# Layer 1 of a two-layer relational graph attention kernel: eleven Strassen pairs and three plain tiles instead of ten and five, with q's edge work moved among the products

## The chip, the cores and the metric

One core of one Trainium2 chip. The time is the device time of one execution in microseconds (us); where several runs are told of, their median. TensorE (PE) does matrix products and transposes, VectorE (DVE), ScalarE (ACT) and GpSimd (POOL) work element by element, SyncE (SP) issues transfers. Each engine works its own list of instructions in order and waits for others by semaphores.

## The reference, cut to what matters

N = 3125 nodes of 768 numbers, E = 53125 edges (src, dst, one of R = 3 relations), float32 throughout. Two attention layers, a residual and a layer norm. Layer 1 has H = 4 heads of 192 columns, layer 2 one head of 768:

```python
xr = einsum('nd,rdf->rnf', x, W)              # every node by each relation's 768x768 matrix
qi, kj = xr[etype, dst] @ q, xr[etype, src] @ k
alpha = leaky_relu(qi + kj, 0.2)
e = exp(alpha - segment_max(alpha, dst)[dst])
out = segment_sum(e / z[dst] * xr[etype, src], dst) + b      # z: sum of e over a node's edges
h = elu(layer1(x)); out = layernorm(x + layer2(h))
```

## The kernel before, in words

**Tiles.** Nodes stand in NT = 25 tiles of 125. Edges, sorted by dst, are padded into 440 steps of 128, and for the softmax they lie as 110 rows of 512 (`ROWS`, `RL`), each row on a partition.

**The tables.** Before xr is known, each node's q and k scores for the three relations come from x times (W q) and (W k), into `qk_node`. POOL scatters the q part, one indirect transfer for each of the 25 tiles (`q_scattered`), into a table in DRAM of zeros, one line of 12 numbers (3 relations x 4 heads) an edge. SP then loads that table whole (`big<-q_fill`, 110 rows of 512 x 12 numbers), and DVE spreads it over the edges: `q_ends` runs one scan over each of the 12 columns, PE turns the rows' last values (`turn_q_ends`), DVE carries them from row to row (`q_carries`), PE turns them back (`turn_q_carry`), and `q_of_edges` adds them in by 12 instructions of 512 columns, masks each relation's four columns by the edge's relation (3 of 2048) and sums the relations into `alpha` (2 of 2048).

**The product phase of layer 1** makes xr. `PLAINS` tiles are done plainly by `dense`: six units (3 relations x 2 halves of 384 columns), each of 6 products over chunks of 128 rows. The other tiles go in `PAIRS`, two at a time, by Strassen's scheme: for each relation 7 products of 3 chunks (`product`), written as A11, S2, S1, A12, S3, S4, A22 in the order list `ORDER`, interleaved so that two relations overlap; a pair is a turn of 21 products (j = 0 to 20 in the first). The scheme needs sums of the pair's four quarters (`sum_x`, four DVE instructions of 375 columns) and of each relation's weight quarters (`sum_w`, three of 1152 columns, and `sum_w_in_place`, one). After each product ACT copies it out (A11, A12) or DVE adds it to what is there (`add_product`, all others); PE's next product into the same bank waits for that: S3 for the add of S2, S4 for that of S1, A22 for that of S3, S2 of the relation after next for that of A22.

In layer 1 the five plain tiles come first. PE runs `turn_rows` in tile 0 and, in tile 3, `turn_q_ends` behind unit 0 and `turn_q_carry` behind unit 2. After tile 4 it waits for `qcarry_taken` and enters the pairs. DVE does in this order: `q_ends`, `sum_w(0)`, `q_carries`, `q_of_edges`, `found_tiles` (14 small instructions), `sum_w` of relations 1 and 2, one `place_hot`, `sum_x(0)`, the sums in place, and then goes along `ORDER`. Between products PE also looks up k values by one-hot products (`look_up`, 24 groups of three, one group in seven products), and DVE picks from them (`select`). POOL meanwhile gathers the other k values from the k table, paced by the count of units and products done (`units_before`).

**The row phase of layer 1**: for 440 steps POOL gathers rows of xr, ACT makes weighted one-hots, PE multiplies, DVE adds into `big`.

**Between the layers**: DVE divides tile t by its softmax sum and adds b + 1 (`divide`), ACT takes exp (`exp_hidden`), DVE forms the ELU (min, max), PE turns the tile (`x_turn`), ACT copies it (`take`), PE makes its q and k (`flat_products`, `flat_turn`), ACT copies those (`take_flat`, `take_nodes`). This is a loop over five turns of U = 5 tiles. ACT stores the k table of five tiles at a time (`store_k`), SP stores the turned tiles (`store_xT`). Layer 2 then goes as layer 1 with 1 plain tile, 12 pairs and one head.

## Time and profile before

| what | us |
|---|---|
| three runs | 2480.73, 2479.11, 2479.05; median 2479.11 |
| the profiled execution: time, span | 2475.89, 2474.2 |
| TensorE busy | 2410.9 (97%) |
| VectorE busy | 1366.4 (55%) |
| ScalarE busy | 1042.4 (42%) |
| GpSimd busy | 1611.6 (65%) |
| mean granted TensorE clock | 0.992 of full speed |

The span runs from the first instruction to the last. Line numbers are those of the kernel before.

### The profile page before, as it was taken

How to read it: one execution, taken by the hardware profiler on the slowest of the kernel's cores; microseconds unless marked ns; L12 is line 12 of the kernel's file. 1: busy time of each engine (PE TensorE's matmuls, PEld its weight loads, DVE VectorE, ACT ScalarE, POOL GpSimd, SP SyncE). 2: the span in 40 equal slices, each digit the busy share in tenths (PEclk: the TensorE clock that was granted, in tenths of full speed). 3: DMA queues.
4: the chain of work that ended last, by engine and by line, in shares of the span. 5: the costliest groups of instructions: out<-in, count | busy, mean ns of one | idle time of the engine just before them, and what ended most of it. 6: DMA issues, size and time to landing. Idle time of an engine off the chain costs nothing.

```text
span 2474.2 us, 42371 instructions
## 1 busy us (share of the span) xinstructions
PE 2410.9 (97%) x10155; PEld 1664.5 (67%) x10155; DVE 1366.4 (55%) x2669; ACT 1042.4 (42%) x2950; POOL 1611.6 (65%) x1672
## 2 busy tenths in 40 slices
PE   8999999999999999999989999999997999999998
PEld 4555666665599999999976566665554555555554
DVE  7537665655588888888897543332331332233232
ACT  0111000000099999999974000000002566666664
POOL 1377777777377777777736766667714777777774
PEclk9999999999999999999999999999999999999999
DMA  7652334332299999999843233322226999999996
GB/s 280 213 141 55 98 103 113 99 83 66 63 315 331 314 312 321 316 312 323 296 146 100 67 87 90 89 73 79 72 68 190 342 337 345 341 337 343 340 332 235
DMA packets 163568, 505.15 MB, mean 204 GB/s; under 512 B 54505, under 2 KB 60178, under 8 KB 163349
## 3 DMA queue, kind: packets, MB, share of 16 engines
q0 software_dynamic: 96048, 354.41, 42.7%
q1 hardware_dynamic: 54449, 143.18, 17.7%
q10 hardware_dynamic: 12962, 6.14, 1.1%
q8 instruction: 63, 1.03, 0.2%
q14 instruction: 46, 0.38, 0.0%
HBM read 424.00 MB, written 79.54 MB: 204 GB/s over the span
## 4 chain that ended last, share of the span: by engine, by line
PE 89%; DVE 4%; DMA 2%; POOL 2%; issue 2%; ACT 0%; ACTq 0%; DVEq 0%; SPq 0%; POOLq 0%
PE banks L1022 36%; PE banks L1064 23%; PE banks L1088 11%; PE banks L1084 11%; PE banks L930 2%; PE banks L732 1%; PE banks L907 1%; POOL q_fill L1472 1%; PE banks L925 1%; PE banks L767 1%; DMA big<-q_fill 1%; PE banks L725 1%; POOL ring L1510 1%; PE banks L743 1%; DVE ring L1552 1%
## 5 line engine op out<-in xcount | busy, mean ns | idle before, releaser
L1510 POOL DMA_INDIRECT ring<-xr_table,row_idx x704 | 667.4, 948 | 303.0 <-PE banks L1064 96.4
L1485 POOL DMA_INDIRECT big<-k_table,row_idx x700 | 687.9, 983 | 259.8 <-issue 208.0
L1286 ACT ACTIVATE work<-work,wE 128x125 f32<-128x125 f32 x1760 | 552.0, 388 | 35.2 <-DVE work L1987 19.5
L1022 PE MATMUL banks<-work 128*125 128x384 f32 x1548 | 534.1, 488 | 1.4 <-DVE work L1840 1.4
L1064 PE MATMUL banks<-ring,work 128*125 128x193 f32 x2816 | 471.4, 327 | 7.5 <-ACT work L1286 7.5
L1064 PEld LDWEIGHTS banks<-ring,work 128*125 128x125 f32 x2816 | 465.0, 188 | 7.7 <-issue 7.7
L2004 DVE TENSOR_TENSOR big<-big,banks 125x772 f32 x440 | 421.7, 958 | 64.9 <-PE banks L1064 55.9
L1862 DVE TENSOR_TENSOR ring<-ring,banks 125x384 f32<-125x384 f32 x330 | 182.2, 553 | 488.5 <-PE banks L1022 487.2
L1022 PEld LDWEIGHTS banks<-work 128*125 128x125 f32 x1548 | 283.5, 188 | 183.8 <-DVE work L1840 2.1
L1022 PE MATMUL banks<-big,work 128*125 128x384 f32 x1152 | 397.8, 487 | 0.0
L1308 ACT ACTIVATE work<-rel,wE 128x125 f32<-128x125 f32 x440 | 216.1, 491 | 234.7 <-PE banks L1088 225.1
L1022 PEld LDWEIGHTS banks<-big,work 128*125 128x125 f32 x1152 | 211.5, 188 | 136.4 <-issue 0.2
L1084 PE MATMUL banks<-ring,work 128*125 128x384 f32 x704 | 286.8, 489 | 13.0 <-DMA ring<-xr_table,row_idx 13.0
L1269 ACT COPY ring<-banks 125x384 f32<-125x384 f32 x66 | 31.6, 479 | 633.5 <-PE banks L1022 633.5
L1088 PE MATMUL banks<-ring,work 128*125 128x386 f32 x704 | 287.2, 490 | 0.0
L2064 DVE TENSOR_SCALAR small<-banks 125x1 f32<-125x1 f32 x25 | 3.9, 158 | 399.8 <-PE banks L1088 399.8
L1084 PEld LDWEIGHTS banks<-ring,work 128*125 128x125 f32 x704 | 131.9, 188 | 112.5 <-issue 18.7
L1510 POOL DMA_INDIRECT work<-xr_table,row_idx x176 | 167.0, 949 | 60.8 <-PE banks L1088 23.7
L1088 PEld LDWEIGHTS banks<-ring,work 128*125 128x125 f32 x704 | 132.2, 188 | 97.0 <-issue 4.5
L1296 ACT ACTIVATE rel<-iota_n,dloc 128x125 f32<-128x125 f32 x440 | 169.1, 384 | 9.2 <-DVEq L1978 7.4
L907 PE MATMUL banks<-work 128*125 128x384 f32 x432 | 140.5, 487 | 0.0
L1265 ACT COPY ring<-banks 125x384 f32<-125x384 f32 x66 | 31.6, 479 | 245.3 <-PE banks L1022 245.3
(282 smaller groups left out, 2005.4 us busy)
## 6 DMA issues: line engine op xcount, KB each, us to landing
xr_table<-ring SPq DMA_DIRECT2D x75, 337.8 KB
xr_table<-ring SPq DMA_DIRECT2D x75, 336.9 KB
work<-in_L_gnn_W SPq DMA_DIRECT2D x36, 384.0 KB, 7.1
ring<-xr_table,row_idx POOLq DMA_INDIRECT x704, 5.0
big<-k_table,row_idx POOLq DMA_INDIRECT x700, 2.4
work<-in_x_turned SPq DMA_DIRECT2D x25, 375.0 KB, 5.6
out<-work SPq DMA_DIRECT2D x25, 336.0 KB
work<-in_x SPq DMA_DIRECT2D x23, 336.0 KB
```

The source lines that it names most:

```text
L907: last = pe.matmul(bank[b][0:TN, 0:n_cols], xT_slot(n if l == 0 else PLAIN_TILE, TN)[:, c, :], w_cols(r, first, n_cols)[:, c, :], start=(c ...
L1022: last = pe.matmul(bank[b][0:TN, 0:HALF], left_side(l, left, pair)[:, c, :], right_side(l, left, r)[:, c, :], start=(left in ("A11", "S1", ...
L1064: last = pe.matmul(bank[2 * slot + half][0:TN, m * HW:(m + 1) * HW], one_hots[l][:, slot, h, :], row[:, half * HB2 + m * HW:half * HB2 + ( ...
L1084: pe.matmul(sums[0:TN, bass.ds(at, HALF)], one_hots[l][:, st % AHEAD, 0, :], row[:, 0:HALF], start=False, stop=False, skip_group_check=True)
L1088: pe.matmul(sums[0:TN, bass.ds(at + 512, ROWW[l] - HALF)], one_hots[l][:, st % AHEAD, 0, :], row[:, HALF:ROWW[l]], start=False, stop=False ...
L1286: last = nc.scalar.activation(one_hots[l][:, slot, h, :], hot[:, slot, :], ACT.Copy, scale=wE[:, bass.ds(st, 1), h:h + 1].rearrange("p a b ...
L1296: nc.scalar.activation(gaps[:, slot, :], iota_n[:, :], ACT.Abs, scale=-1.0, bias=dloc[:, bass.ds(st, 1)]).then_inc(s["gap_set"], 1)
L1308: nc.scalar.activation(one_hots[l][:, j % AHEAD, 0, :], gaps[:, j % AHEAD, :], ACT.Relu, scale=wE[:, bass.ds(st, 1), 1:2].rearrange("p a b ...
L1485: nc.gpsimd.indirect_dma_start(k_at(l, st), None, ktab[l], bass.IndirectOffsetOnAxis(ap=row_idx[:, st:st + 1], axis=0)).then_inc(s["k_gath ...
L1510: nc.gpsimd.indirect_dma_start(row_slot(l, st % GS), None, xrtab[l], bass.IndirectOffsetOnAxis(ap=row_idx[:, st:st + 1], axis=0)).then_inc ...
L1862: nc.vector.tensor_tensor(out_, in_, acc, ALU.add).then_inc(s["halves_out"], 1)
L2004: nc.vector.tensor_tensor(tile, tile, banks[0:TN, 2 * (j % AHEAD):2 * (j % AHEAD) + 2, 0:RWL // 2], ALU.add).then_inc(s["sum_added"], 1)
```

## The change

Layer 1 has three plain tiles and eleven pairs; the last pair is tiles 23 and 24, and pair 0 is loaded into the other slot, before the q table. All spots that are counted in products from the end move on by 21. k lookups and the loads of W2 begin one turn later. The q table is loaded in two halves (256 of each row's 512 edges), and `q_ends` scans half after half. The twelve columns are no longer written apart (`qf`): every later instruction of q works in the loaded table itself, whose neighbours of one column lie 12 numbers (48 bytes) apart. PE's turns of q's ends stand in plain tile 2, behind units 3 and 4. DVE does `sum_w(0)`, two thirds of `sum_w(1)` and `sum_x(0)` ahead of `q_ends`; `q_of_edges` stays ahead of the products, the masks and the sums of q go among the first turn's products, behind j = 2 and j = 7, the rest of the weight sums behind j = 9 to 15, `found_tiles` behind 16, and `sum_x(1)` behind 18. The wait for `qcarry_taken` ahead of the products is gone. Between the layers, b + 1 is formed before the row phase, the softmax sums of the first five tiles are inverted first, tile 0's ELU comes ahead of tile 2's division, ACT looks two tiles ahead instead of three in the first turn, and SP stores layer 2's k table. The last product is followed by one POOL memset of 1152 columns instead of one of 3456.

```diff
-    PLAINS = [U, 1]
+    PLAINS = [3, 1]
-    LOOK_FROM = [0, R]
+    LOOK_FROM = [R, R]
-    Q_ENDS_AT, Q_CARRY_AT, PLACES_FROM = 5, 9, 14
+    Q_ENDS_AT, Q_CARRY_AT, PLACES_FROM = 5, 9, [16, 14]
+    EDGES_AT, ALPHA_SPOT = 2, 7
+    W_SPOTS = [9, 11, 14, 15]
+    X_SPOTS = [18, TURN // 2 + 2]
+    W2_FROM = R
+    SUMMED = [{"S": [1, 2, 5], "S3": [3, 4, 7], "A22": [1, 6, 8]}, {"S": [9, 10, 11], "S3": [12, 13, 14], "A22": [9, 10, 11]}]
...
+                        sp.wait_ge(s["qk_copied"], 2 + U * i + U)
+                        for a, b in PARTS:
+                            sp.dma_start(ktab[l].rearrange("(t p r) h -> p t (r h)", p=TN, r=R)[a:b, bass.ds(U * i, U), :],
+                                         qk_node[a:b, bass.ds(U * i, U), R * H:2 * R * H]).then_inc(s["k_stored"], 16)
...
+                if l == 0:
+                    sp.wait_ge(s["qk_done"], 2 + WT + FLATS)
+                    load_pair(0)
                 sp.wait_ge(s["q_scattered"], 16 * NT * (l + 1))
...
+                    half = RL // 2 * R * H
+                    sp.dma_start(q_filled(l)[:, 0:half], q_rows[:, 0:half]).then_inc(s["q_loaded"], 16)
+                    sp.dma_start(q_filled(l)[:, half:], q_rows[:, half:]).then_inc(half_loaded, 16)
...
                     if k == 1:
+                        sp.wait_ge(s["dense_done"], 2 * UNITS + 2 * UNITS)
                         load_pair(1)
-                        sp.wait_ge(s["dense_done"], 2 * UNITS + 2 * UNITS)
-                        load_pair(0)
+                        for row, arr in ((q2_row, q2), (k2_row, k2)):
+                            sp.dma_start(row, arr.rearrange("f h -> (f h)").partition_broadcast(P)).then_inc(qk_loaded, 16)
...
-                    meets = {0: {2: turn_rows}, 3: {0: turn_q_ends, 2: turn_q_carry}} if l == 0 else {}
+                    meets = {0: {2: turn_rows}, 2: {3: turn_q_ends, 4: turn_q_carry}} if l == 0 else {}
                     dense(k, meets.get(k, ()))
-                if l == 0:
-                    pe.wait_ge(s["qcarry_taken"], l + 1)
...
-                        if k == 0 and not first:
-                            store_k(i - 1)
...
-                qs = qf if l == 0 else raw
+                qs = raw
...
+                    mid = RL // 2 if l == 0 else RL
                     for q in range(R * H):
-                        link(nc.vector.tensor_tensor_scan(qs[:, q, :], same[0:ROWS, :], raw[:, q, :], 0.0, ALU.mult, ALU.add))
+                        link(nc.vector.tensor_tensor_scan(qs[:, q, 0:mid], same[0:ROWS, 0:mid], raw[:, q, 0:mid], 0.0, ALU.mult, ALU.add))
+                    if l == 0:
+                        dve.wait_ge(half_loaded, 16)
+                        for q in range(R * H):
+                            link(nc.vector.tensor_tensor_scan(qs[:, q, mid:], same[0:ROWS, mid:], raw[:, q, mid:],
+                                                              qs[:, q, mid - 1:mid], ALU.mult, ALU.add))
...
                 if l == 0:
-                    place_hot(0)
-                    dve.wait_ge(s["dense_done"], 2 * UNITS + UNITS * 3)
-                sum_x(0)
-                if l == 1:
+                    sum_w(0)
+                    sum_w_firsts(1).then_inc(s["w_summed"], 1)
+                    dve.wait_ge(s["w_summed"], 2)
+                    sum_x(0)
+                    q_firsts()
+                    q_ends()
+                    sum_w_in_place(0)
+                    q_carries()
+                    sum_w_in_place(1)
+                    q_of_edges()
+                else:
...
                 for j, (left, u) in enumerate(ORDER[l]):
                     if left not in BY_ACT:
                         add_product(left, u)
-                    if j % TURN == TURN // 2 + 2 and l < j // TURN + 1 < PAIRS[l]:
+                    if j % TURN == X_SPOTS[0 if l == 0 and j < TURN else 1] and l < j // TURN + 1 < PAIRS[l]:
                         sum_x(j // TURN + 1)
+                    if l == 0 and j == EDGES_AT:
+                        q_of_relations()
+                    if l == 0 and j == ALPHA_SPOT:
+                        q_sums()
+                        dve.sem_inc(s["k_taken"], 2)
+                    if l == 0 and j == W_SPOTS[0]:
+                        sum_w_firsts(2).then_inc(s["w_summed"], 1)
+                    if l == 0 and j == W_SPOTS[1]:
+                        sum_w_last(1)
+                    if l == 0 and j == W_SPOTS[2]:
+                        sum_w_in_place(2)
+                    if l == 0 and j == W_SPOTS[3]:
+                        dve.wait_ge(s["w_summed"], SUMMED[0]["S"][2])
+                        sum_w_last(2)
...
+                    take_weights(0, U)
+                    for t in range(2):
+                        divide(t, brow[0:TN, :]).then_inc(s["u_ready"], 1)
+                    for t in range(U):
+                        activate(t, t)
+                        if t == U - 2:
+                            take_weights(U, NT)
+                        divide(t + 2, brow[0:TN, :]).then_inc(s["u_ready"], 1)
```

`sum_w_firsts` is the first two instructions of `sum_w`, `sum_w_last` the third, `q_of_relations` the three masks, `q_sums` the two sums. `take_weights(a, b)` adds a small number to the softmax sums of tiles a to b and inverts them, `activate` is the ELU's min and max.

## Rows read from the trace of the kernel before

**Rows 1.** The trace in stretches: length, busy time of each engine, clock, DMA.
```profile
core 0: us, PE busy (x) PEld busy (x) DVE busy (x) ACT busy (x) POOL busy (x), PEclk, DMA share, GB/s
210.80:214.52 3.72, 3.72 (x13) 2.22 (x12) 3.22 (x14) 1.34 (x3) 2.81 (x4) 1.00 0.44 136
...
1362.50:1877.00 514.50, 513.59 (x1743) 308.62 (x1741) 190.82 (x352) 35.54 (x74) 307.01 (x320) 1.00 0.27 78
```
**Rows 2.** Timeline of TensorE in layer 1's plain tiles: start, length, instructions, idle before.
```profile
181.01 0.25 PE L938 MATMUL banks<-ident,small 110*12 110x110 f32 x1 [2.18 <-DVE small L1687]
...
189.10 35.10 PE L907 MATMUL banks<-work 128*125 128x384 f32 x108
225.64 2.20 PE L1022 MATMUL banks<-work 128*125 128x384 f32 x6 [1.45 <-DVE work L1840]
```
**Rows 3.** The chain that ended last: start, length, what.
```profile
146.38 19.18 DMA big<-q_fill
...
1671.46 89.04 PE banks L1022 x276
```
**Rows 4.** Timeline of VectorE on q in layer 1.
```profile
165.59 15.07 DVE L1686 TENSOR_TENSOR_SCAN big<-same,big 110x512 f32<-110x512 f32 x12 [38.23 <-DMA big<-q_fill]
...
189.55 9.42 DVE L1706 SCALAR_TENSOR_TENSOR big<-big,small 110x512 f32<-110x512 f32 x12 [0.17 <-DVE small L1703]
199.00 6.95 DVE L1710 SCALAR_TENSOR_TENSOR big<-rel,big 110x2048 f32<-110x2048 f32 x3
```
**Rows 5.** VectorE by line and shape, layer 1: count, busy us, mean ns.
```profile
L1862 DVE TENSOR_TENSOR ring<-ring,banks 125x384 f32<-125x384 f32 x150 | 82.8, 553 | 174.2 <-PE banks L1022 173.3
...
L1686 DVE TENSOR_TENSOR_SCAN big<-same,big 110x512 f32<-110x512 f32 x12 | 14.7, 1224 | 38.6 <-DMA big<-q_fill 38.2
...
L1706 DVE SCALAR_TENSOR_TENSOR big<-big,small 110x512 f32<-110x512 f32 x12 | 9.0, 752 | 0.6 <-DVE small L1703 0.2
...
L1837 DVE TENSOR_TENSOR work<-work 128x375 f32<-128x375 f32 x10 | 5.5, 548 | 0.3
...
L1725 DVE TENSOR_TENSOR big<-work 128x1152 f32<-128x1152 f32 x3 | 4.1, 1355 | 0.4 <-DVE big L1746 0.3
...
L1970 DVE COPY wE<-banks 128x440 f32<-128x440 f32 x4 | 3.6, 897 | 0.4 <-DVE wE L1970 0.2
...
L1688 DVE TENSOR_TENSOR_SCAN big<-same 110x512 f32<-110x512 f32 x1 | 1.2, 1217 | 0.0
```
**Rows 6.** The same view of layer 2, 1382 to 1400 us.
```profile
L1706 DVE SCALAR_TENSOR_TENSOR big<-big,small 110x512 f32<-110x512 f32 x3 | 2.8, 929 | 0.2 <-DVE small L1703 0.2
```
**Rows 7.** Timeline of VectorE: scans of 128 columns.
```profile
593.28 1.80 DVE L1881 TENSOR_TENSOR_SCAN big<-pen,big 110x128 f32<-110x128 f32 x4
...
599.52 2.04 DVE L1881 TENSOR_TENSOR_SCAN big<-pen,big 110x128 f32<-110x128 f32 x4
```
**Rows 8.** Stretches behind layer 1's last product, columns as in rows 1.
```profile
675.70:678.00 2.30, 0.43 (x5) 0.22 (x3) 2.01 (x4) 0.00 (x0) 2.30 (x1) 1.00 0.58 181
...
680.00:683.00 3.00, 0.00 (x0) 0.00 (x0) 2.21 (x6) 1.93 (x7) 2.39 (x3) 0.73 0.51 138
683.00:684.00 1.00, 0.38 (x1) 0.39 (x2) 0.62 (x2) 1.00 (x5) 0.70 (x2) 0.50 0.71 142
...
688.00:690.00 2.00, 2.00 (x13) 2.00 (x12) 1.46 (x3) 1.10 (x5) 1.39 (x3) 0.95 0.99 326
```
**Rows 9.** Timeline between the layers.
```profile
1264.95 0.78 DVE L2013 RECIPROCAL small<-small 125x100 f32<-125x100 f32 x1
...
1266.48 4.04 DVE L2022 SCALAR_TENSOR_TENSOR big<-big,small,brow 125x192 f32<-125x192 f32 x12 [0.15 <-DVE brow L2016]
...
1271.44 1.51 PE L725 MATMUL banks<-ident,work 125*128 125x125 f32 x6 [7.90 <-DVE work L2038]
...
1294.20 1.45 PE L732 MATMUL banks<-work 128*6 128x125 f32 x12 [0.86 <-ACT qk_node L1147]
...
1332.07 1.45 PE L732 MATMUL banks<-work 128*6 128x125 f32 x12 [0.40 <-ACT qk_node L1147]
```

More of the change, by code:

```diff
@@ L1175, in x_turns @@
                             take(t + 1, (k + 1) % U)
+                        if first and k == U - 1:
+                            exp_hidden(t + 3, (k + 3) % U)
                         take_flat(t, k)
@@ L1716, in q_of_edges, with w_sums, sum_w_firsts @@
                     dve.sem_inc(s["q_used"], 1)
-                def sum_w(r):
+                def w_sums(r):
+                    return [w_sum(l, r, i) for i in range(3)]
+                def sum_w_firsts(r):
                     if l == 0:
```

175 lines of the change are left out of this document (92 added, 83 removed).

## The prediction, made before the changed kernel was run

> **What bounds the kernel now.** I read first the engines' shares, then the chain that ended last, then the timelines where the chain leaves TensorE. PE is busy for 97% of the span, and the chain runs over its products. In the product phase a product of three chunks takes 89.04 / 46 = 1.936 us [rows 3]. In the plain tiles 108 recorded products take 35.10 us, so a tile (72 of them) takes 23.4 us and one of its six units 3.90 us [rows 2]. So time is to be won only by taking work from PE or by filling its gaps. Around the change there are three gaps: 2.18 us at the turn of q's ends and 1.45 us ahead of the pairs [rows 2], and, between the layers, a late start and four short stalls [rows 9]. The reader should also see how near q's work stands to the path: the table's load takes 19.18 us from 146.38 [rows 3], DVE waits for it and then scans for 15.07 us [rows 4]. Until now plain tiles of PE covered nearly all of that.
>
> **Part 1, PE's own work.** Two plain tiles go, 46.8 us; one pair comes, 21 products, 40.7 us: -6.1 us. The two old gaps go with the place they stood in: -3.6 us. Together -9.8 us (rounded terms). The 24 groups of lookups only move.
>
> **Part 2, the wait in plain tile 2.** Counting units back from 178.83 (where PE fell idle, 2.18 us before 181.01 [rows 2]), unit 3 of tile 2, three units earlier, ends at 178.83 - 3 x 3.90 = 167.1. PE then waits for `qend_ready`. The load begins when the scatters are through, as before. If its halves land evenly, the first is there at about 156.0 and the second at 165.6 [rows 3]. A scan of 128 columns takes 0.45 us with a constant and 0.51 us with a tensor as its first value [rows 7], one of 512 takes 1.256 with its gap [rows 4]; between them, 256 columns take 0.72 and 0.78. The first half is scanned by 164.6, the second from 165.6 to 174.9, and with the copy 174.7 to 175.1 is the time of the ends. PE waits 7.5 us (7.6 to 8.0 by this sum, less if the second half lands sooner). Lower bound: the table wholly there by 152, then DVE alone needs 18 us, 170.2, a wait of 3.1; upper bound 8.3. Behind PE's wait stand units 4 and 5 and the whole product phase; DVE's `q_of_edges` waits behind unit 4 as well.
>
> **Part 3, the clock.** Behind layer 1's last product PE falls idle at about 676.1. From 680 to 683 its mean clock is 0.73, so it went from 2.4 to 1.2 GHz at about 681.4, after 5 us; PE resumes at 683.62, and is at 2.4 GHz again at about 688.2 [rows 8]. Those 4.6 us at half speed cost 2.3 us. A wait of 7.5 us is longer than those 5 us: +2.3 us. With a wait under 5 us it is nothing.
>
> **Part 4, the first turn of pairs.** Here DVE gets new work at a new price: q's instructions read and write numbers 48 bytes apart. A plain instruction of 1152 columns takes 1.355 us and one of 375 takes 0.548, so 1.04 ns a column and 0.16 fixed [rows 5]. A step of 12 bytes (layer 2) takes 0.929 instead of 0.752 for 512 columns [rows 5, 6], 0.35 ns a column more. A copy that writes 440 numbers 16 bytes apart takes 0.897 us, 1.68 ns a column, 0.64 more [rows 5]. No row shows such an instruction at 48 bytes except the scan, which reads at that step for 1.224 against 1.217 [rows 5]; but it needs 2.1 ns a column anyway and can hide the step. I take the price of 16 bytes, the nearest row. Then, with old prices in brackets [rows 4]: twelve of `q_of_edges` 13.2 to 13.4 us (9.42), three masks 10.9 (6.95), two sums 7.3 (4.6 at the masks' rate).
>
> The Trainium skill bears on this (Advanced Engine Details and Errata, Memory Cachelines): SBUF has lines of 16 bytes, and an access pattern that goes to another line with each access pays. By it 48 bytes should cost what 16 bytes cost; by the scan's row the step would be free. The first gives the sum below, the second the 3.8 us named beside it.
>
> Now the walk, in us from the first product's start; a product 1.94, an add 0.55, `sum_x` 2.3, two thirds of a weight sum 2.7, one third 1.4 [rows 3, 5]. The carries are turned one unit earlier, -3.9; DVE ends `q_of_edges` at 9.7. S3 (j = 4, due at 7.7) needs the add of S2: 10.3, a stall of 2.5. The masks run from 10.8 to 21.8, then the add of S3; A22 (j = 9, due at 20.0) starts at 22.4: 2.4. Two adds, the sums of q to 30.8, two adds, two thirds of `sum_w(2)` to 34.6; S2 of the third relation (j = 13, due at 30.1): 4.5. The last product of the turn ends at 46.2; DVE has just finished `found_tiles` (3.7 us [rows 1]) and one-hots, adds that product (that alone must follow it) and does `sum_x(1)`: A11 of pair 1 starts at 49.8: 3.6. Sum +13.0 us. At 12 bytes' price the same walk gives 8.4, at the contiguous one 3.8, nearly all `sum_x(1)` behind j = 18. None of these stalls reaches 5 us, so no clock is lost. Layer 1's front: -9.8 + 7.5 + 2.3 + 13.0 = +13.0 us.
>
> **Part 5, between the layers.** DVE does three tiles' divisions (12 in 4.04 us) before the first ELU; now two, -1.35. Inverting 20 numbers instead of 100 saves 0.6 of 0.78 us and its gap, and b + 1 leaves the 0.75 us between that and the first division: PE's first turn comes 2.5 us sooner, the second tile's 2.3, and from there PE runs on [rows 9]. Given back: ACT makes up its extra exp at the first turn's end, and DVE inverts the other 80 numbers there: +0.6, an estimate between nothing and 1.3. The four stalls of PE behind ACT's k stores (0.86 to 0.40, first and last in rows 9, four in all, 3.0 us) go, with 0.2 us of refilling. Sum -5.0 us (-3 to -6.5). b + 1 now stands between the last product and the first one-hots; ACT has its first set ready 1.2 us before PE starts at 683.62 on the first gathered rows, which covers it; without that cover it is +0.6. SP's k stores make the next turned tile wait a tile or so, but its slot is wanted five tiles later: nothing. The shorter memset: POOL then waits for the last stores anyway: nothing. The last sixteen k gathers are let go 14 products (27 us) before PE turns them instead of 17, and keep POOL busy for 16 us by the page (983 ns each): nothing, but with less to spare. The later q2 and k2 rows are read three groups later than before: nothing.
>
> **Sum.** +13.0 - 5.0 = +8.0 us on the profiled execution (2475.89, span 2474.2), 2483.9. The three runs shown have a median of 2479.11, 3.2 above that one; the change is set against the median: **2487.1 us**.
>
> **The rivals.** (a) The step costs only what 12 bytes cost: front -9.8 + 7.5 + 2.3 + 8.4 = +8.4, total +3.4, 2482.5. For it: no row shows more at a small step. Against it: the 16-byte copy. Chance 0.2. (b) The step is free, as for the scans: +3.8 in the turn, total -1.2, 2477.9. Chance 0.12. (c) The other side: the products have room for all of q's work, so that turn 1 costs nothing, total 8.0 - 13.0 = -5.0, or somewhat below, since a late DVE would then also be no reason for `sum_x(1)` to hold PE: 2474 and less, faster. For it: layer 2 does the same edge work among its products, and PE is busy there for 513.59 of 514.50 us [rows 1]. Against it: that is one head's work, 3 columns and not 12. It decides from where the turn's stalls stay under 0.5 us in all; at the walk's contiguous price they are already 3.8. Chance 0.13. (d) The step of 48 bytes is dearer than one of 16, 2 ns a column: some 2 us more on `q_of_edges`, 2 on the masks and 1.3 on the sums, of which the walk passes on nearly all, total about +13, 2492. Chance 0.1. The forecast itself keeps 0.45.
>
> **Numbers.** A change under 0.2% (5 us) can't be told from none by this kernel's measurement. Faster: (c) and a little of (b), 0.15. Same: (a), most of (b), the lower end of the forecast, 0.35. Slower: 0.5. Range 2474 to 2492: from (c)'s edge to (d). The likeliest case's own range, from the bounds of the wait, the clock and part 5, is 2481 to 2491.
>
> **What would show it.** In the profile after: PE idle behind a plain unit at about 167 until about 175, released by DVE's copy of the ends, and half clock behind it; `q_of_edges` near 1.1 us each and the masks near 3.6; stalls of PE in the first turn at its fifth, tenth, fourteenth and twenty-second product; the row phase starting 13 us later; then the first turned tile 2.5 us nearer to the row phase's end, no stall at each fifth tile. Wrong if the masks take 2.3 us, if the table lands well before 160, or if the first turn shows no stall.

## The result and the profile after

The changed kernel takes 2494.96 us (median of six runs, 2492.03 to 2498.96) against 2479.72 for the kernel before in the same job: ratio 1.0066, 95% interval 1.0056 to 1.0076, so +16.4 us, slower. The profiled execution took 2498.96 us, its span is 2497.2, its mean clock 0.984. It is the slowest of the six, and the profile of before is one of the faster ones.

First the timeline of PE behind plain tile 2 and in the first turn of pairs (start, length, what, and in brackets the idle time before it and who ended it); it answers to [rows 2]. L956 turns q's ends, L925 are the plain tiles, L1038 the products, L948 the lookups.

```profile
181.42 0.34 PE L956 MATMUL banks<-ident,small 110*12 110x110 f32 x1 [8.14 <-DVE small L1709]
181.55 6.06 PE L925 MATMUL banks<-work 128*125 128x384 f32 x12
...
203.09 5.59 PE L1038 MATMUL banks<-work 128*125 128x384 f32 x12 [3.52 <-DVE ring L1895]
...
215.60 2.17 PE L1038 MATMUL banks<-big,work 128*125 128x384 f32 x6 [1.11 <-DVE ring L1895]
...
228.03 6.78 PE L1038 MATMUL banks<-big,work 128*125 128x384 f32 x12 [4.45 <-DVE big L1759]
...
246.27 3.48 PE L1038 MATMUL banks<-work 128*125 128x384 f32 x6 [3.73 <-DVE work L1873]
249.54 4.49 PE L1038 MATMUL banks<-big,work 128*125 128x384 f32 x12
...
255.81 0.67 PE L948 MATMUL banks<-qk_node,big 125*128 125x300 f32 x2
```

PE waits 8.14 us for the ends, and in the turn 3.52, 1.11, 4.45 and 3.73 us ahead of its fifth, tenth, fourteenth and twentieth product, 12.8 us in all. The second thing to see is what stands behind the waits: twelve recorded products take 4.03 us at full clock (4.14 in the plain tiles), but 6.06 behind the wait for the ends and 5.59 and 6.78 behind two of the waits in the turn, and six take 3.48 instead of 2.10. The stretches of the same timeline show the clock (length, busy time by engine, then PE's granted clock, 1.00 being 2.4 GHz and 0.50 being 1.2):

```profile
181.40:187.60 6.20, 6.18 (x14) 3.27 (x14) 3.00 (x5) 0.00 (x0) 4.98 (x5) 0.66 0.05 1
203.09:208.60 5.51, 5.51 (x13) 3.20 (x14) 5.47 (x3) 0.00 (x0) 4.90 (x3) 0.73 0.02 0
228.03:234.70 6.67, 6.67 (x13) 3.65 (x14) 2.23 (x3) 0.00 (x0) 5.15 (x6) 0.60 0.16 33
246.27:249.60 3.33, 3.33 (x7) 1.84 (x8) 0.00 (x0) 0.00 (x0) 2.72 (x3) 0.62 0.06 2
```

DVE's groups by shape from 150 to 262 us (busy time, mean ns of one, idle before) answer to [rows 4] and [rows 5]:

```profile
L1731 DVE SCALAR_TENSOR_TENSOR big<-big,small 110x512 f32<-110x512 f32 x12 | 13.8, 1152 | 0.6 <-DVE small L1728 0.2
L1737 DVE SCALAR_TENSOR_TENSOR big<-rel,big 110x2048 f32<-110x2048 f32 x3 | 11.5, 3822 | 0.1
...
L1742 DVE TENSOR_TENSOR big<-big 110x2048 f32<-110x2048 f32 x1 | 3.8, 3823 | 0.0
L1744 DVE TENSOR_TENSOR big<-big 110x2048 f32<-110x2048 f32 x1 | 3.8, 3817 | 0.0
```

At the 48-byte step `q_of_edges` takes 1.15 us an instruction (0.75 before), a mask 3.82 (2.3), a sum 3.82 (2.29): 0.75 to 0.78 ns a column more than contiguous, so about 1.8 ns instead of 1.04.

A place that I had not looked at is POOL's scatters of q, while DVE does the sums that were moved ahead of `q_ends`. Timeline of both engines:

```profile
132.56 1.36 DVE L1758 TENSOR_TENSOR big<-work 128x1152 f32<-128x1152 f32 x1
132.82 2.16 POOL L1487 DMA_INDIRECT q_fill<-qk_node,start_at  x1 [0.30 <-issue]
...
135.28 1.18 POOL L1487 DMA_INDIRECT q_fill<-qk_node,start_at  x1 [0.30 <-issue]
135.35 1.36 DVE L1764 TENSOR_TENSOR big<-work,big 128x1152 f32<-128x1152 f32 x1
...
136.62 1.35 DVE L1758 TENSOR_TENSOR big<-work 128x1152 f32<-128x1152 f32 x1
136.77 2.26 POOL L1487 DMA_INDIRECT q_fill<-qk_node,start_at  x1 [0.30 <-issue]
```

The two scatters that began 0.26 and 0.15 us behind the start of one of DVE's sums of 1152 columns took 2.2 us instead of 1.19; the one at 135.28, which began 0.07 us ahead of a sum, took 1.18, and that sum its usual 1.36. From the first product of the plain tiles to the issue of q's load there are 46.7 us (106.00 to 152.69); before there were 43.8 (102.61 to 146.38).

Between the layers, the chain that ended last (start, length, what) has the row phase and layer 2's plain tile here, and PE's timeline its first turned tile:

```profile
710.01 579.96 PE banks L1080 x3520
...
1361.49 23.42 PE banks L925 x72
```

```profile
1295.42 1.51 PE L743 MATMUL banks<-ident,work 125*128 125x125 f32 x6 [5.46 <-DVE work L2092]
...
1307.41 0.86 PE L743 MATMUL banks<-ident,ring 125*128 125x125 f32 x6 [0.71 <-DVE ring L2092]
...
1310.92 0.86 PE L743 MATMUL banks<-ident,work 125*128 125x125 f32 x6 [1.06 <-DVE work L2092]
```

From the row phase's start to layer 2's first plain unit: 651.5 us, before 655.5 (683.62 to 1339.15): -4.05. PE's wait ahead of the first turned tile is 5.46 us instead of 7.90 [rows 9].

So the two traces, whose spans differ by 23.0 us, part like this: 3.4 us up to the first plain product, 22.8 from there to the first lookup behind the first turn (149.8 us against 127.0), nothing from there to the end of PE's last instruction of layer 1's product phase (446.5 in both), -3.9 from there to layer 2's first plain product, +0.7 behind it.

### The profile page after: what moved, and what is told of

The parts are those of the page before. It is cut to its first block, busy times and chain, and to the rows that moved or that the text cites. A ratio compares the mean times of both kernels' runs of the same rounds, so it can differ in the third digit from the quotient of the medians.

```text
span 2497.2 us, 42356 instructions
## 1 busy us (share of the span) xinstructions
PE 2419.6 (97%) x10137; PEld 1665.5 (67%) x10137; DVE 1392.8 (56%) x2702; ACT 1040.6 (42%) x2944; POOL 1626.1 (65%) x1673
## 4 chain that ended last, share of the span: by engine, by line
PE 90%; DVE 5%; DMA 2%; POOL 2%; issue 1%; DVEq 0%; ACT 0%; SPq 0%; ACTq 0%; POOLq 0%
PE banks L1038 36%; PE banks L1080 23%; PE banks L1104 11%; PE banks L1100 11%; PE banks L948 1%; PE banks L785 1%; PE banks L750 1%; POOL q_fill L1487 1%; PE banks L925 1%; PE banks L943 1%; PE banks L743 1%; PE banks L761 1%; DVE ring L1568 1%; DMA work<-xr_table,row_idx 1%; DVE big L1731 1%
## 5 line engine op out<-in xcount | busy, mean ns | idle before, releaser
L1500 POOL DMA_INDIRECT big<-k_table,row_idx x700 | 695.9, 994 | 277.7 <-issue 203.1
L1038 PE MATMUL banks<-work 128*125 128x384 f32 x1620 | 561.4, 489 | 7.3 <-DVE work L1873 3.7
L1895 DVE TENSOR_TENSOR ring<-ring,banks 125x384 f32<-125x384 f32 x345 | 190.2, 553 | 502.2 <-PE banks L1038 500.4
L1038 PEld LDWEIGHTS banks<-work 128*125 128x125 f32 x1620 | 298.1, 188 | 200.7 <-issue 6.5
L1038 PE MATMUL banks<-big,work 128*125 128x384 f32 x1206 | 419.4, 490 | 5.6 <-DVE big L1759 4.5
L1038 PEld LDWEIGHTS banks<-big,work 128*125 128x125 f32 x1206 | 223.2, 189 | 151.8 <-issue 5.3
L1104 PEld LDWEIGHTS banks<-ring,work 128*125 128x125 f32 x704 | 132.1, 188 | 97.4 <-issue 5.2
L2047 DVE TENSOR_SCALAR work<-iota_n,dloc 128x125 f32<-128x125 f32 x444 | 130.2, 294 | 0.6 <-DVE big L2053 0.3
```

Of the source, the lines that this page charges most:

```text
L1038: last = pe.matmul(bank[b][0:TN, 0:HALF], left_side(l, left, pair)[:, c, :], right_side(l, left, r)[:, c, :], start=(left in ("A11", "S1", ...
L1104: pe.matmul(sums[0:TN, bass.ds(at + 512, ROWW[l] - HALF)], one_hots[l][:, st % AHEAD, 0, :], row[:, HALF:ROWW[l]], start=False, stop=False ...
L1500: nc.gpsimd.indirect_dma_start(k_at(l, st), None, ktab[l], bass.IndirectOffsetOnAxis(ap=row_idx[:, st:st + 1], axis=0)).then_inc(s["k_gath ...
L1895: nc.vector.tensor_tensor(out_, in_, acc, ALU.add).then_inc(s["halves_out"], 1)
L2047: nc.vector.tensor_scalar(hot[:, slot, :], iota_n[:, :], dloc[:, bass.ds(st, 1)], None, ALU.is_equal).then_inc(s["hot_built"], 1)
```

## The experiments

One yardstick serves throughout, because PE's first 100 us vary from run to run, whatever the kernel (the first plain product starts at 99.7 to 106.0 us in the runs told of here): the time from the issue of q's load to the first lookup behind the second product that follows the first turn (in the kernel before: behind its second product). It is 83.2 us before (146.38 to 229.61) and 103.1 after (152.69 to 255.81). By the forecast's terms it should have been 83.2 - 9.8 + 7.5 + 2.3 + 13.0 = 96.2. Each kernel was timed against the kernel before on one chip, and kernels are compared here by these ratios; a ratio's own interval is 0.0009 to 0.0016 either way where times can be read at all, so a difference between two kernels is known to some 3 to 4 us only, and the traces have to say where it lies.

Theory: the front costs 20 us, by DVE's work at the 48-byte step, by the clock that PE loses behind each stall, by `sum_x(1)` standing behind `found_tiles`, and by the scatters; the part between the layers gives 4 back. Rivals: DVE's amount of work or its order and not the step; the clock as a side effect that hides behind DVE.

**1. The part between the layers alone, on the kernel before.** SP's stores, ACT's order, DVE's order and b + 1 as in the change; nothing of layer 1's front.

```diff
-                    for k in range(3):
+                    for k in range(2):
                         exp_hidden(k, k, first=True)
...
+                    take_weights(0, U)
+                    for t in range(2):
+                        divide(t, brow[0:TN, :]).then_inc(s["u_ready"], 1)
+                    for t in range(U):
+                        activate(t, t)
```

> The kernel before with the edits between the layers alone (b + 1 ahead of the row phase, the softmax sums of the first five tiles inverted first, tile 0's ELU ahead of tile 2's division, ACT two tiles ahead in the first turn, SP stores layer 2's k table). Theory, from the trace after: these edits are worth 4 to 5 us, since the row phase ends 26.4 us later than before and layer 2's products only 22.3 us later. So this kernel takes 4 to 5 us less than the kernel before (about 2475), PE's first turned tile comes 2.4 us nearer to the last add, and the stall at each fifth tile is gone. Rival: the edits give back what they save (ACT's extra exp, the second inversion, SP's queue), and the front costs only what was forecast; then this kernel is within 1 us of the kernel before or slower.

Measured: 2475.16 us against 2478.96, ratio 0.9989 (0.9980 to 0.9998), so -2.7 by the ratio (0.5 to 5.0) and -3.8 by the medians. Its chain:

```profile
688.33 580.24 PE banks L1068 x3520
...
1340.08 23.42 PE banks L911 x72
```

651.75 us between the two, 3.8 less than before: the theory holds, and the part is worth 3 to 4 us, a little less than the 4 to 5 expected. This run tells something else too. Its front is that of the kernel before, yet the row phase starts 4.7 us later than in the profile of before, and only 2.7 of that stand in the first 105 us. In its timeline PE waits 3.66 us at the turn of q's ends and not 2.18 [rows 2], and the 24 recorded products behind it take 9.61 us and not 7.92:

```profile
183.94 0.25 PE L942 MATMUL banks<-ident,small 110*12 110x110 f32 x1 [3.66 <-DVE small L1692]
184.03 9.61 PE L911 MATMUL banks<-work 128*125 128x384 f32 x24
```

A wait well under 5 us had cost clock. Its yardstick is 85.0 us, 1.8 more than in the profile of before.

**2. The step alone.** The changed kernel, with the instructions behind the scans on a contiguous view of the same table. The scans still write at the 48-byte step, so these instructions find the numbers in the wrong places and the result is not the reference's; the count of instructions and of numbers is the same.

```diff
+                near = q_filled(l).rearrange("r (q x) -> r q x", q=R * H) if l == 0 else raw
...
-                        link(nc.vector.scalar_tensor_tensor(out=qs[:, q, :], in0=q_first, scalar=c_in[:, q:q + 1],
-                                                            in1=qs[:, q, :], op0=ALU.mult, op1=ALU.add))
+                        link(nc.vector.scalar_tensor_tensor(out=near[:, q, :], in0=q_first, scalar=c_in[:, q:q + 1],
+                                                            in1=near[:, q, :], op0=ALU.mult, op1=ALU.add))
```

> The changed kernel, but the carries' twelve instructions, the three masks and the two sums of q read and write the loaded table as if each column stood contiguous (the scans keep the 48-byte step). The numbers in it are then in the wrong places, so alpha is not the reference's; the count of instructions and of numbers is unchanged. Theory, the step is what costs: the twelve fall from 1.19 to 0.79 us each, the masks from 3.84 to 2.32, the sums from 3.82 to 2.29, 12.5 us of DVE in all; the stalls of PE at the fifth, tenth and fourteenth product (3.5, 1.1, 4.5 us) go to under 1 us each, that at the twentieth stays, and with the clock that the stalls cost the kernel takes 11 to 14 us less than the changed one, 2482 to 2485. Rival, the amount of work or its order costs and not the step: the durations stay or fall, and the time stays within 3 us of the changed kernel's, since found_tiles and sum_x(1) are late in either case.

Measured: 2481.51 us, ratio 1.0013 (1.0004 to 1.0022), 13.1 us less than the changed kernel. DVE's groups and the only stall left in the turn:

```profile
L1732 DVE SCALAR_TENSOR_TENSOR big<-big,small 110x512 f32<-110x512 f32 x12 | 9.0, 752 | 0.6 <-DVE small L1729 0.2
...
L1738 DVE SCALAR_TENSOR_TENSOR big<-rel,big 110x2048 f32<-110x2048 f32 x3 | 6.9, 2290 | 0.1
...
L1743 DVE TENSOR_TENSOR big<-big 110x2048 f32<-110x2048 f32 x1 | 2.3, 2331 | 0.0
```

```profile
229.48 2.20 PE L1038 MATMUL banks<-work 128*125 128x384 f32 x6 [3.73 <-DVE work L1874]
```

The theory holds; the rival (amount or order) falls. 12.4 us less of DVE's time take 14.3 us from the yardstick (88.8), because the stalls take the half clock behind them with them. The stall ahead of the twentieth product stays, 3.73 us as before, and this time without half clock behind it.

**3. `sum_x(1)` sooner.** `X_SPOTS = [18, ...]` becomes `[15, ...]`, so that it stands ahead of `found_tiles`.

> The changed kernel with sum_x(1) behind j = 15 instead of j = 18, so ahead of found_tiles. Theory: the stall of 3.7 us at the twentieth product is of DVE's order alone: sum_x(1) stands behind found_tiles (4.3 us) though nobody waits for found_tiles before the lookups of the next turn. It goes, or shrinks to the 1 us that an add now waits for found_tiles, and with it the half-speed stretch of 2 us: 4 to 6 us less than the changed kernel, about 2491. Rival: DVE is behind by a fixed amount of work and the stall only moves to the eighteenth or nineteenth product, which waits for an add: within 2 us of the changed kernel.

Measured: 2490.01 us, ratio 1.0048 (1.0034 to 1.0062), 4.5 us less than the changed kernel by the ratio, and 4.1 less in the yardstick (99.0). In its timeline the stall ahead of the twentieth product is gone and no other has come:

```profile
178.30 0.34 PE L956 MATMUL banks<-ident,small 110*12 110x110 f32 x1 [11.27 <-DVE small L1709]
...
225.38 7.08 PE L1038 MATMUL banks<-big,work 128*125 128x384 f32 x12 [4.44 <-DVE big L1759]
...
236.16 5.97 PE L1038 MATMUL banks<-work 128*125 128x384 f32 x18
241.96 4.03 PE L1038 MATMUL banks<-big,work 128*125 128x384 f32 x12
...
247.77 0.67 PE L948 MATMUL banks<-qk_node,big 125*128 125x300 f32 x2
```

Its first row matters too. The wait for the ends is 11.27 us here and 10.69 in experiment 2, with the changed kernel's own front up to there, against 8.14 in the profile after. PE came later to the wait in that profile: in plain tile 0 it had waited 2.00 us for `turn_rows` and then run at half clock, so that the 156 recorded products behind took 51.85 us, and 50.49 in these two runs:

```profile
119.86 0.34 PE L900 MATMUL banks<-ident,wE 110*128 110x110 f32 x1 [2.00 <-DVE small L1641]
...
121.43 51.85 PE L925 MATMUL banks<-work 128*125 128x384 f32 x156
```

**4. The clock.** Products that nobody reads stand in PE's four waits, so that PE has work there.

```diff
+                def fill(n, left_):
+
+                    for i in range(n):
+                        pe.matmul(bank[SOFT][0:TN, 0:HALF], left_[:, i % 3, :], w_quarter(0, 0, 0)[:, i % 3, :],
+                                  start=True, stop=True)
```

> The changed kernel with products that nobody reads put into PE's four waits: 22 of 384 columns (7.1 us) ahead of the turn of q's ends, 8, 11 and 8 (2.6, 3.6, 2.6 us) ahead of the fifth, fourteenth and twentieth product. They fit into the waits of 8.1, 3.5, 4.5 and 3.7 us. Theory: the waits also cost clock, because PE runs at half speed behind each; with PE at work in them the clock stays at 2.4 GHz. Behind the first wait this gives 2.1 us, behind the fourteenth product 2.9, behind the twentieth 2.1; what it gives behind the fifth product (1.7) is taken again by the wait at the tenth, where DVE's masks set the time. Sum: 7 us less than the changed kernel, about 2489. Rival: the stalls alone are the loss and the clock is a side effect that hides behind DVE's work: the time is that of the changed kernel within 2 us, or more by what the products add.

Measured: 2500.58 us, ratio 1.0092 (1.0077 to 1.0108). I had mis-sized it: each such product is two recorded instructions and takes 0.65 us, so the work was 32 us and not 16 and overran the waits. It says little, except that with 12 us of overrun the loss against the changed kernel was 6. With the sizes right:

> The same as the kernel with products nobody reads in PE's four waits, but with the sizes right: a product of 384 columns over one chunk takes 0.65 us (two recorded instructions), so 11, 4, 5 and 4 of them (7.1, 2.6, 3.2 and 2.6 us) and not twice as many, which overran the waits by some 9 us. Theory, the waits cost clock as well: with the overrun gone the first lookup of the second turn stands at about 245 instead of 252.8, and the kernel takes 6 to 8 us less than the changed one, 2487 to 2489. Rival, the clock hides behind DVE's work: the time of the changed kernel, 2495, within 2 us.

This run and ten others fell on chips where the kernel before itself took 2776 to 2816 us and its runs spread by 45 to 61 us: a few us can't be told there (here 2790.43 against 2780.45, ratio 1.0036, 1.0003 to 1.0069; a second timing of the same kernel 1.0011, 0.9981 to 1.0041), but up to the first lookups their traces can mostly be read. The yardstick is 97.8 us here. In the second timing it is 103.6, no better than the changed kernel's; there DVE waits 4.33 and 3.61 us around the turns of the carries, for nothing that the trace names, where it waits nothing and 1.26 us on the quiet chip. A third timing, on a quiet chip:

> The changed kernel with 11, 4, 5 and 4 unread products in PE's four waits. Theory (a wait costs the half-speed stretch behind it too): 5 us less than the changed kernel, ratio to the kernel before 1.0045 against 1.0066. Rival (the clock hides behind DVE): 1.0066 within 0.0008.

Measured: 2489.47 us against 2478.23, ratio 1.0043 (1.0029 to 1.0057), 5.7 us less than the changed kernel; yardstick 97.4. The unread products stand at L958:

```profile
169.06 7.26 PE L958 MATMUL banks<-work 128*125 128x384 f32 x22
179.48 0.25 PE L966 MATMUL banks<-ident,small 110*12 110x110 f32 x1 [3.15 <-DVE small L1721]
179.57 4.05 PE L927 MATMUL banks<-work 128*125 128x384 f32 x12
...
199.09 4.11 PE L1050 MATMUL banks<-work 128*125 128x384 f32 x12 [0.94 <-DVE ring L1907]
...
211.59 3.59 PE L1050 MATMUL banks<-big,work 128*125 128x384 f32 x6 [2.58 <-DVE ring L1907]
...
224.32 4.03 PE L1050 MATMUL banks<-big,work 128*125 128x384 f32 x12
```

With PE at work in the waits, the twelve recorded products behind them take 4.05, 4.11 and 4.03 us instead of 6.06, 5.59 and 6.78. So the clock's share of the loss is real: keeping it in all four waits gives 5.3 to 5.7 us, about 2 of them behind the wait for the ends, which the forecast had. The rival falls as a whole and holds in one place: what PE gains behind the fifth product it waits for at the tenth, where DVE's masks set the time (2.58 us instead of 1.11). And the row at 211.59 is odd: 2.58 us of idleness, and yet half clock for most of six recorded products.

**5. DVE's sums held back** until the scatters are through.

```diff
+                    dve.wait_ge(s["q_scattered"], 16 * NT)
                     sum_w(0)
```

> The changed kernel, but DVE holds sum_w(0), the first two thirds of sum_w(1) and sum_x(0) until q's scatters are through (until then it did them at 132.6 to 142.6, beside POOL's scatters). Theory: DVE's moved work slows the scatters' issue. In the trace after, the 25 scatters start from 111.4 to 150.1, 38.7 us, two of them taking 2.2 instead of 1.19 us and four 1.3 to 1.4; before, 108.0 to 143.8, 35.8 us, all at 1.19. Held back, they take 35.8 again, q's table lands 2.5 to 2.9 us sooner, all of DVE's chain with it, and the kernel takes 2 to 3 us less. DVE's 9 us of sums fit between the scatters' end and the first half's landing (10 us), with 1 us to spare or over. Rival: the load of pair 0 slows them (it is issued ahead of them), then the scatters still take 38.7 us and the time is the same or 1 us more.

Measured on one of the wide-spreading chips, so in its time inconclusive (2785.69 against 2780.45, ratio 0.9986, 0.9949 to 1.0022), and once more so:

> The same kernel as the one in which DVE holds its first sums until q's scatters are through, timed again for the same reason. In its first trace the 25 scatters started over 36.4 us instead of 38.7. Theory: 2 to 3 us less than the changed kernel, 2492 to 2493. Rival: the front is not bound by the table's landing, and the time stays at 2495.

(2773.22 against 2778.13, ratio 1.0002, 0.9970 to 1.0035.) The traces do tell. The scatters' row (durations in ns, least, median, most; then the first and the last start), first of the changed kernel, then of this one's second run:

```profile
L1487 POOL DMA_INDIRECT q_fill<-qk_node,start_at x25: 1182/1187/2262, 111.4 to 150.1; - x25
```

```profile
L1487 POOL DMA_INDIRECT q_fill<-qk_node,start_at x25: 1182/1187/1232, 107.6 to 143.5; - x25
```

38.7 us become 35.9, as in the kernel before (108.0 to 143.8); in this kernel's first run they become 36.4. The sums beside them account for 2.3 us: 1.0 at each of two scatters and 0.16 at each of two more. The rest is a few scatters of 1.3 to 1.4 us around 120, which that first run has as well. From the first plain product to the load's issue there are 43.8 to 44.4 us in the five runs with the sums held (these two and the three of 7), and 46.5 to 46.9 in the eight that keep the change's order; pair 0's load is issued ahead of the scatters in all thirteen. So 2 us and more of the scatters' 2.9 are DVE's doing, and the rival (the pair's load) falls. From the first plain product to the first lookup behind the turn it is 148.0 and 147.8 us instead of 149.8, so 1.8 to 2.0 us of it arrive there; that they reach the end of the kernel is shown only together with the others, in 7.

**6. The table in one load**, scanned by twelve scans of 512.

> The changed kernel with q's table loaded by one transfer and scanned by twelve scans of 512 instead of twenty-four of 256. Theory: whole, the table takes 19.2 us to land and 15.1 to scan, 34.3 from issue to the ends; in halves it took 28.4 (152.69 to 181.10). So PE's wait in plain tile 2 grows by 6 us and DVE's chain is 6 us later: 6 us more than the changed kernel, 2501. Rival: the two transfers only share the same engines and the split saves nothing (or the front isn't bound by the table at all): within 2 us of the changed kernel.

Its time can't be read (2785.12 against 2780.45, ratio 1.0021, 0.9984 to 1.0059), but the scans can. They start 20.2 us after the load's issue (148.5):

```profile
168.67 15.09 DVE L1702 TENSOR_TENSOR_SCAN big<-same,big 110x512 f32<-110x512 f32 x12 [30.06 <-issue]
183.79 0.17 DVE L1703 COPY small<-big 110x12 f32<-110x12 f32 x1
```

From the issue to the ends 35.3 us; in halves 28.4 to 29.6 in the runs read here. The halves are worth the 6 us that were expected, in DVE's chain. How much of it reaches the lookups can't be told: the yardstick is 112.6, but DVE also waits 7.14 us at the turn of the carries, for nothing that the trace names.

**7. What the change would be with three of these mended**: sums held, `sum_x(1)` behind j = 15, and 11, 4 and 5 unread products in the waits. Its first two timings fell on the other chips (1.0050, 1.0015 to 1.0084, and 1.0048, 1.0018 to 1.0077); the expectations of the first and of the last:

> The changed kernel (eleven pairs, three plain tiles) with all that helped: DVE's first sums held until q's scatters are through, sum_x(1) behind j = 15, unread products in the waits at the turn of q's ends (11), at the fifth product (4) and at the fourteenth (5). Theory: -2.5, -5 and -4 to -5 us of clock, 2482 to 2484, so still slower than the kernel before, because the 48-byte step's 12.5 us of DVE stay. Rival: the three gains are the same time counted three times (DVE's chain sets the end whatever PE does in its waits), and the kernel ends at 2488 to 2490.

> The changed kernel with DVE's first sums held until q's scatters are through, sum_x(1) behind j = 15, and 11, 4 and 5 unread products in PE's waits. Theory, from its two traces (93.0 and 94.9 us from the issue of q's load to the first lookup against 103.1, and 2.3 to 2.9 us less ahead of it): 11 to 12 us less than the changed kernel, so 2 to 5 us above the kernel before, ratio 1.001 to 1.002. Rival (one loss counted three times, or what is won is lost at a later wait): 6 us less, ratio 1.004.

Measured the third time: 2484.09 us against 2478.23, ratio 1.0023 (1.0014 to 1.0032), 10.7 us less than the changed kernel, a little under what was expected (11 to 12) and well above the rival's 6. The three add up within the intervals; the yardstick is 95.3 us. The 5.7 us by which this kernel is still above the one before are less than the step was worth in experiment 2 (13 us), and ahead of its tenth product PE still waits 2.57 us behind masks and adds. That a free step would bring it below the kernel before is likely, but the two were not run together.

**8. A kernel of five plain tiles with what was good.** The kernel before, with the edits between the layers and the table in halves, and 32 small unread products in PE's wait of 7.6 us ahead of layer 1's row phase. The last of these was first put in alone:

> The kernel before with the edits between the layers and, in PE's wait of 7.6 us ahead of layer 1's row phase, 32 small products that nobody reads (ident by iota_n, 125 columns, some 0.21 us each, 6.8 us). Theory, a wait costs its own length and then the half-speed stretch behind it: PE starts the row phase at 2.4 instead of 1.2 GHz, and this kernel takes 2 us less than the same without them (2475.2), 2473. Rival: the first rows come no faster than the gathers give them, so the clock behind this wait is worth nothing; the time is the same within 1 us.

(2777.87 against 2780.45, ratio 0.9949, 0.9906 to 0.9992, on a wide-spreading chip; the interval is too wide to tell the theory from the rival.) Then all three:

> Ten pairs and five plain tiles as before, with the edits between the layers, the 32 unread small products ahead of layer 1's row phase, and q's table loaded and scanned in halves into the contiguous copy. Theory: the halves give q's ends 5.5 to 6 us sooner (34.3 against 28.4 us from issue to ends), so that PE's waits at the turn of q's ends (2.2 us before, 3.7 in the run with the edits between the layers alone) and ahead of the pairs (1.4) go, -3.6 to -5; the row phase starts at full clock, -2.3. Sum: 6 to 7 us less than the 2475.2 of the edits between the layers alone, 2468 to 2469, and 10 less than the kernel before. Rival: PE's wait ahead of the pairs is set by DVE's sum of work and not by the table; then only the clock's 2 us come, 2473.

Its three timings fell on such chips (ratios 1.0001, 0.9988 and 1.0011, each within 0.004). The trace of the second showed why the halves gave little: the ends were ready at 176.2, PE turned them at 178.96, but the carries only at 186.90, behind unit 2 of plain tile 3, because that is their place in PE's list; DVE's chain began at 188.7, 41.7 us behind the load's issue (43.2 before), and PE waited 3.00 us ahead of the pairs. The yardstick was 83.6, as before. So the rival was right there, by another road. One more edit:

```diff
-                    meets = {0: {2: turn_rows}, 3: {0: turn_q_ends, 2: turn_q_carry}} if l == 0 else {}
+                    meets = {0: {2: turn_rows}, 3: {0: turn_q_ends, 1: turn_q_carry}} if l == 0 else {}
```

> The five-tile kernel with the edits between the layers, q's table in halves and 32 unread small products ahead of layer 1's row phase, and the turn of the carries behind unit 1 of plain tile 3 instead of behind unit 2. Theory: in the last trace DVE had the carries at 182.9 or sooner but PE turned them at 186.9, so a fixed place in PE's list took back what the halves gave. One unit sooner (3.9 us), DVE ends sum_x(0) 3.9 us sooner and PE's wait ahead of the pairs (3.0 us, and half clock behind it) goes: from the issue of q's load to the first lookup 80 us or less, against 83.2 in the kernel before, and 2467 to 2469 in all. Rival: the carries come ready only behind unit 1 (sum_w(0) stands ahead of them in DVE's list), PE waits there instead, and nothing is won over the last one.

Measured on a quiet chip: 2465.43 us (2464.86 to 2469.28) against 2476.04, ratio 0.9957 (0.9943 to 0.9970): 10.7 us less than the kernel before by the ratio, 27 less than the changed one. PE's timeline:

```profile
175.97 0.26 PE L949 MATMUL banks<-ident,small 110*12 110x110 f32 x1
...
180.04 0.22 PE L954 MATMUL banks<-ident,flag 12*110 12x12 f32 x1
180.19 38.97 PE L918 MATMUL banks<-work 128*125 128x384 f32 x120
218.99 2.10 PE L1033 MATMUL banks<-work 128*125 128x384 f32 x6
...
222.86 0.67 PE L941 MATMUL banks<-qk_node,big 125*128 125x300 f32 x2
```

```profile
671.82 4.75 PE L1060 MATMUL banks<-iota_n,ident 128*125 128x125 f32 x42
678.10 1.57 PE L1077 MATMUL banks<-ring,work 128*125 128x193 f32 x8 [1.53 <-DMA ring<-xr_table,row_idx]
```

No wait at the turns, none ahead of the pairs, yardstick 77.9. Ahead of the row phase (L1060 are the unread products, of which this view shows the last 42 records of 64) the wait is 1.53 us, and eight recorded products of 193 columns take 1.57 us, so at full clock from the first. That is worth little, though. From the end of layer 1's product phase to layer 2's first plain product there are 658.6 us, against 659.3 with the edits between the layers alone and 663.0 before: PE's first row product stands 8.7 us behind that phase and not 7.6, which takes back more than half of the 1.9 us that the clock gives. So of the 10.7 us some 5.3 are the front's, 3.7 the edits' between the layers, and under 1 the unread products'. By this trace the rival of the first expectation here (worth nothing within 1 us) was right.

## Why the prediction was right and wrong

**Right: the side, the stalls and most terms.** The masks and sums at the price of a small step, four stalls in the first turn (3.5, 1.1, 4.5 and 3.7, sum 12.8 us; forecast 2.5, 2.4, 4.5 and 3.6, sum 13.0), and the half clock behind the wait for the ends (2.0, forecast 2.3). The fourth stall stands at the twentieth product, not the twenty-second: the walk's own 46.2 is six products behind the fourteenth, and only the words there ("the last product of the turn") are wrong. "16 bytes, the nearest row" was a good choice: 1.8 ns a column, where it gave 1.68. The Trainium skill's rule of 16-byte lines (Advanced Engine Details and Errata, Memory Cachelines), by which 48 bytes should cost what 16 cost, agrees to within some 8% here (by the 16-byte row 1.68 ns a column, measured 1.8).

**Right by luck.** The wait for the ends was 8.14 us, forecast 7.5, but in the runs of experiments 2 and 3 it was 10.7 and 11.3: the scatters made the ends some 2.9 us late, and in the profile after PE happened to be as late, by a longer wait and half clock in plain tile 0. And the sum of the stalls agrees better than its parts: the first is 1.0 us longer than forecast, and the half clock behind it (1.6 us) filled part of the wait at the tenth product.

**Wrong: "None of these stalls reaches 5 us, so no clock is lost"** (part 4), and "With a wait under 5 us it is nothing" (part 3). The time to the fall was read from one place, behind layer 1's last product [rows 8], and taken for a threshold. Behind stalls of 3.5 to 4.5 us the products of the first turn took 6.1 us more than at full clock (1.56 + 2.75 + 1.38 + 0.46, each against 4.03 or 2.10). The first of these was covered by the wait at the tenth product, so that some 4.6 us were the clock's net cost in the turn. Keeping PE at work in all four waits, the one for the ends included, gave 5.3 us back in the trace and 5.7 in the time. This is the step that failed, and the largest part of the miss.

**Left out: what DVE's moved work does beside POOL.** Part 2 says "The load begins when the scatters are through, as before", and part 4's walk costs the sums moved ahead of `q_ends` at nothing. They stand beside the scatters, which take 2.9 us longer in all, 2.3 of them by these sums, and the table's landing sets everything behind it. The Trainium skill states it (SBUF — State Buffer, Who interferes with whom): a VectorE instruction with two SBUF inputs contends with a GpSimd instruction that reads SBUF. The scatters' instructions read `qk_node` and `start_at`, the sums read two quarters. The trace agrees for the scatters that began behind a sum's start (2.2 us instead of 1.19); where the scatter began first, neither it (1.18) nor the sum (1.36) took longer. I had not looked there.

**Over-sized: part 5.** -5.0 forecast; -4.05 in the trace after, and in the run with that part alone -3.8 in the trace and -2.7 to -3.8 in the time. The first turned tile came 2.44 us nearer (forecast 2.5); but in the first turn of five PE then waits 0.71 and 1.06 us for ELUs, where +0.6 had been put down.

The sum with the measured terms: 8.0 + 4.6 (the clock in the turn, net) - 0.3 (the clock behind the ends) + 1.4 (the turn's stalls, 12.8 and the 1.6 that was covered, against 13.0) + 0.6 (the wait for the ends) + 2.9 (scatters) + 1.0 (part 5) = 18.2, against 16.4 by the ratio. The 1.8 that is left over was not traced to a place; a likely part of it is that the profile of before, on which the forecast stands, had a luckier front than usual: the run of experiment 1, whose front is the same kernel's, has a yardstick 1.8 us longer, with a wait of 3.66 us and half clock behind it.

**The rivals.** (a) and (b) needed a cheaper step, and it measured 1.8 ns a column; (c) needed room among the products, and the turn's stalls were 12.8 us. Experiment 2 stands for (b)'s condition, a free step, and is still 3 us slower than the kernel before: (b)'s 2477.9 lacks the same two terms. (d), a dearer step, comes nearest in its total (+13 against +16.4), but by chance: the step is dearer than 16 bytes by 0.1 ns a column and not by 0.3, and what makes up its total is the clock and the scatters.

## What to carry to other kernels

A stall of the matmul engine costs its own length and often a half-speed stretch behind it, and short stalls can do this too: price both. A slow stretch costs nothing where the next wait is set by another engine anyway. Where a wait can't be removed, unread products in it are worth trying (5.7 us in layer 1's front, under 1 ahead of the row phase). When an engine's work is moved into a gap, look at what the other engines do in that gap: the gap of one was the critical stretch of another. And when something is made ready sooner, look for the fixed place in the consumer's list that still waits for nothing: the halves gave nothing (yardstick 83.6 against 83.2) until the turn of the carries was moved too (77.9).

## What the runs showed of the hardware that was not expected

- The clock fell to half behind waits of 3.52, 3.73 and 4.45 us in the profile after, 3.66 in experiment 1, 2.57 to 2.60 in the runs with unread products, and 2.00 in plain tile 0 of the profile after; it did not behind waits of 3.73 in experiment 2, 3.15 in experiment 4 and 2.18 in the profile of before. So the length of the wait alone does not tell it; no rule is drawn here.
- A plain DVE instruction whose numbers lie 48 bytes apart takes 1.8 ns a column, against 1.04 contiguous, 1.39 at 12 bytes and 1.68 for the copy at 16. A scan of 256 at that step takes 0.69 to 0.75 us without its gap; the forecast, from scans of 128 and 512 columns, had 0.72 and 0.78 with it.
- A scatter issued by POOL took 2.2 to 2.4 us instead of 1.19 where it began 0.05 to 0.3 us behind the start of one of DVE's sums of 1152 columns with two inputs, in all eight traces with the change's order; where it began together with a sum or just ahead of it, it took 1.18 or 1.19.
- On the chips with the wide spread, six of the seven three-tile kernels waited 5.8 to 7.2 us for the last k gathers ahead of their turn (0.3 us on the others), and the five-tile ones did not: the 14 products of lead left in part 5, "nothing, but with less to spare", are enough only where the gathers run at their usual pace.
